# Turning token rows and gated rows on VectorE instead of TensorE in a mixture-of-experts feed-forward

## The chip, the cores and the metric

The kernel runs on one core of a Trainium2 chip. Its time is device microseconds of that core, from launch to end. Engines are TensorE (PE), VectorE (DVE), ScalarE (ACT), GpSimd (POOL) and SyncE (SP); each follows its own instruction stream, and they wait for each other on semaphores. DMAs issued from SP, ACT and POOL queues share 16 DMA engines.

## The reference

```python
def reference(x, ctx_2048, ...):                     # both (16, 512, 1024) fp32
    # long convolution of products k_i*k_j of 8-channel heads, contracted with the queries
    x = x + xattn(ctx, ctx, layernorm(x), ssm_kernel, D, 8)
    # mixture of experts: 32 routed experts, 8 of them per row, and a shared one
    h = layernorm(x).reshape(-1, 1024)               # T = 8192 token rows
    scores = sigmoid(h @ router_w)                   # (T, 32)
    # groups of 4 experts, 4 groups masked out, top 8 of the rest, weights scaled by 2.5
    gate = ragged_dot(xs, w_gate, group_sizes)       # xs: rows sorted by expert; w_gate (32, 1024, 512)
    up   = ragged_dot(xs, w_up, group_sizes)
    down = ragged_dot(silu(gate) * up, w_down, group_sizes)      # w_down (32, 512, 1024)
    routed = (down[unsort].reshape(T, 8, 1024) * weight).sum(1)
    shared = silu(h @ sw_gate) * (h @ sw_up) @ sw_down           # inner width 1024
    return x + routed + shared
```

## The kernel before, in words

Three parts run one after the other. `mix_and_route` computes the convolution and the router, and writes normed token rows to DRAM (`xnd`), the residual to `x2d`, and for each expert a list of its token numbers to `lists`. `plan` turns the counts into a table of tiles. `feed_forward` (L1009) does the rest, and only it is changed in its order of work.

It walks 672 tiles of 128 rows: 544 routed tiles (`EXPERT_TILES`), each of one expert, then twice 64 tiles of the shared expert, whose inner width is taken in two halves (`SH0`, `SH1`). The walk (`walk_tiles`, L988) is a few single tiles and loops of two. In tile t each engine also does work of its neighbours, so the stages overlap: the token rows of t+1 and t+2, the down product of t-1. The order is written out by hand in each engine's `tile`.

fp32 products are three passes (`three`, L1313): high with high, high with low, low with high, where the high part is a copy to fp32r and the low part is what is left. So every operand comes as a pair: whi and wlo of the weights (from `raw`), xhi and xlo of the token rows, hhi and hlo of the gated rows. ACT makes the high parts, DVE the low ones.

A tile goes like this. POOL loads the list row (`load_list`, L1109) and gathers 128 token rows into one of two `xg` buffers (`gather`, L1115). PE turns them with eight transposes into the PSUM tile xps (L1325); ACT and DVE make xhi and xlo from it (`x_high`, L1190, `x_low`, L1261). PE multiplies gate and up, 48 matmuls of 512 columns into gps and ups (L1336 to L1339). ACT applies silu (L1200), DVE multiplies with ups (L1282): the gated rows hb. PE turns them with four transposes into hps (L1358), ACT and DVE make hhi and hlo (L1212, L1299), and PE does the down product, 24 matmuls into yps, one tile later (L1349 to L1353). ACT and DVE copy yps to yrow, and POOL scatters it to `yd` (L1160).

PE's order within `tile(t)` is: gate and up of t, transposes of token rows t+1, down of t-1, transposes of gated rows t. ACT's is silu of t, x_high of t+1, the weight split of the next expert if t+1 is its first tile (`split_gu`, L1177), the copy of half of yps, hhi, and `split_dn`. DVE follows with the same pieces. Each expert's weights are 12 chunks in one `raw` buffer; SP loads the next expert's chunk once both engines have split the present one (L1068 to L1084).

In the 128 shared tiles `fetch_picks` (L1124) gathers four of a token's eight routed rows per tile into four `picked` buffers, `add_picks` (L1266) adds them to yrow with their weights, then yps is added (L1292), and ACT stores the sum (L1221).

## Time and profile before

| | us |
|---|---|
| median of 3 runs | 15433.22 (15427.76 to 15435.76) |
| the profiled execution, span from first to last instruction | 15412.0 |
| PE busy | 14528.9 (94%) |
| VectorE, ScalarE, GpSimd busy | 6313.4 (41%), 3173.3 (21%), 3896.2 (25%) |
| mean DMA rate | 94 GB/s |

The profile page gives no time of its own for the profiled execution beyond the span; the median of the runs lies 21 us above it. Busy shares are means over stages: the first 3,380 us are the convolution and the router, the rest is the feed-forward. A busy PE is a stream of matmuls whose starts lie close together; how long one occupies the array is read from the distance of starts, not from its own duration.

### The profile page before, as it was taken

The page shows a single profiled execution, that of the slowest core. Times are in us where ns is not written, and L with a number is a line of the kernel's source. Part 1 is how long each engine was busy: PE and PEld are TensorE (multiplying, and loading weights), DVE is VectorE, ACT ScalarE, POOL GpSimd, SP SyncE. Part 2 cuts the span into 40 slices and gives each one's busy share as a digit, 9 for nine tenths or more (in the row PEclk, how much of TensorE's full clock was granted, in tenths as well). Part 3 has the DMA queues.
Part 4 walks back from the last instruction along what each step waited for, and adds up shares of the span by engine and source line. Part 5 has one row for each costly group of instructions (what it writes and reads, how often), then busy time and mean ns, then how long its engine had stood idle before and what let it go on. Part 6 is the DMA issues. An engine that isn't in the chain of part 4 may idle for free.

```text
span 15412.0 us, 212654 instructions
## 1 busy us (share of the span) xinstructions
PE 14528.9 (94%) x73632; PEld 12344.4 (80%) x73633; DVE 6313.4 (41%) x7679; ACT 3173.3 (21%) x4006; POOL 3896.2 (25%) x3973
## 2 busy tenths in 40 slices
PE   7878877749999999999999999999999999999999
PEld 7777777738888888888888888788888888888888
DVE  8998989941221222212221222322212111444554
ACT  3333333311111112211211222312111111111111
POOL 3344445541111111111111111111111111333333
PEclk9888888869999999999999999999999999999999
DMA  2233332241221222212221222322212111666666
GB/s 69 69 63 66 66 64 63 53 72 60 74 75 59 74 76 105 91 60 73 91 74 58 91 89 91 129 93 102 73 60 75 58 60 42 210 206 204 208 204 204
DMA packets 481191, 1445.61 MB, mean 94 GB/s; under 512 B 94385, under 2 KB 94385, under 8 KB 480834
## 3 DMA queue, kind: packets, MB, share of 16 engines
q0 software_dynamic: 286720, 890.00, 17.3%
q1 hardware_dynamic: 172738, 485.33, 11.5%
q10 hardware_dynamic: 21504, 67.13, 1.1%
q8 instruction: 156, 2.56, 0.1%
q14 instruction: 73, 0.60, 0.0%
HBM read 1037.89 MB, written 421.08 MB: 95 GB/s over the span
## 4 chain that ended last, share of the span: by engine, by line
PE 77%; DVE 0%; DMA 0%; issue 0%; ACT 0%; DVEq 0%; ACTq 0%; SPq 0%; POOLq 0%; POOL 0%
PE gps L1318 24%; PE ups L1318 24%; PE yps L1318 24%; PE xps L1325 4%; PE hps L1358 2%; DVE wlo L1246 0%; DMA raw<-in_L_ffn_w_up_dram 0%; ACT whi L1181 0%; DMA xg<-xnd,idx 0%; DVE yrow L1272 0%; DMA picked<-yd,gidx 0%; ACTq L1063 0%; DVEq L1063 0%; DVE xlo L1246 0%; DVE hlo L1246 0%
## 5 line engine op out<-in xcount | busy, mean ns | idle before, releaser
L1282 DVE TENSOR_TENSOR hb<-hb,ups 128x512 f32<-128x512 f32 x672 | 462.1, 688 | 6196.1 <-ACT hb L1200 6196.1
L1160 POOL DMA_INDIRECT yd<-yrow,yidx x544 | 575.6, 1058 | 7816.9 <-DVE yrow L1296 7816.9
L1318 PE MATMUL gps<-whi,xhi 128*128 128x512 f32 x5376 | 2157.4, 401 | 32.8 <-DVE wlo L1246 29.1
L1318 PE MATMUL ups<-whi,xlo 128*128 128x512 f32 x5376 | 2112.9, 393 | 0.0
L1318 PE MATMUL gps<-wlo,xhi 128*128 128x512 f32 x5376 | 2111.6, 393 | 0.0
L1318 PE MATMUL ups<-whi,xhi 128*128 128x512 f32 x5376 | 2111.3, 393 | 0.0
L1318 PE MATMUL gps<-whi,xlo 128*128 128x512 f32 x5376 | 2110.9, 393 | 0.0
L1318 PE MATMUL ups<-wlo,xhi 128*128 128x512 f32 x5376 | 2094.3, 390 | 0.0
L750 PE MATMUL yps<-khi,thi 128*128 128x288 f32 x4608 | 1481.8, 322 | 337.7 <-ACT ysb L436 193.8
L1200 ACT ACTIVATE hb<-gps 128x512 f32<-128x512 f32 x672 | 402.4, 599 | 6729.3 <-PE ups L1318 6719.1
L1318 PE MATMUL yps<-whi,hhi 128*128 128x512 f32 x5376 | 1725.9, 402 | 4.5 <-DVE hlo L1246 4.5
L1318 PE MATMUL yps<-wlo,hhi 128*128 128x512 f32 x5376 | 1674.5, 393 | 0.0
L1318 PE MATMUL yps<-whi,hlo 128*128 128x512 f32 x5376 | 1666.7, 391 | 0.0
L750 PE MATMUL yps<-klo,thi 128*128 128x288 f32 x4608 | 1427.1, 310 | 0.0
L750 PE MATMUL yps<-khi,tlo 128*128 128x288 f32 x4608 | 1419.4, 308 | 0.0
L750 PEld LDWEIGHTS yps<-khi,thi 128*128 128x128 f32 x4608 | 934.9, 203 | 379.2 <-ACT ysb L436 215.9
L1318 PEld LDWEIGHTS gps<-whi,xhi 128*128 128x128 f32 x5376 | 1011.8, 188 | 234.8 <-DVE wlo L1246 30.1
L1318 PEld LDWEIGHTS yps<-whi,hlo 128*128 128x128 f32 x5376 | 1009.4, 188 | 230.3
L1318 PEld LDWEIGHTS ups<-wlo,xhi 128*128 128x128 f32 x5376 | 1010.2, 188 | 228.2
L1318 PEld LDWEIGHTS gps<-whi,xlo 128*128 128x128 f32 x5376 | 1010.7, 188 | 227.5
L1318 PEld LDWEIGHTS yps<-wlo,hhi 128*128 128x128 f32 x5376 | 1009.9, 188 | 222.1
L1318 PEld LDWEIGHTS gps<-wlo,xhi 128*128 128x128 f32 x5376 | 1011.4, 188 | 213.3
(161 smaller groups left out, 20294.0 us busy)
## 6 DMA issues: line engine op xcount, KB each, us to landing
raw<-in_L_ffn_w_gate_dram SPq DMA_DIRECT2D x128, 512.0 KB, 6.0
raw<-in_L_ffn_w_up_dram SPq DMA_DIRECT2D x128, 512.0 KB, 7.6
raw<-in_L_ffn_w_down_dram SPq DMA_DIRECT2D x64, 1024.0 KB, 6.9
cin<-in_ctx_dram SPq DMA_DIRECT2D x64, 512.0 KB, 5.0
xin<-in_x_dram SPq DMA_DIRECT2D x64, 512.0 KB
traw<-kpad SPq DMA_DIRECT2D x64, 512.0 KB, 4.2
xres<-in_x_dram SPq DMA_DIRECT2D x256, 128.0 KB, 2.6
x2d<-xres SPq DMA_DIRECT2D x64, 512.0 KB
```

Of the source, the lines that this page charges most:

```text
L750: last = pe.matmul(yps[j % 2][:, lb % 2, 0:NH], tt[sl][:, c], kk[half][:, lb - d, :], start=(d == 0 and i == 0), stop=(d == lb and i == 2))
L1160: pool.indirect_dma_start(out=yd, in_=yrow[i][:, :], in_offset=None, out_offset=bass.IndirectOffsetOnAxis(ap=yidx[i][:, 0:1], axis=0), bou ...
L1200: act.activation(hb[:, :], gps[:, :], ACT.Silu).then_inc(silu_done, 1)
L1282: dve.tensor_tensor(hb[:, :], hb[:, :], ups[:, :], ALU.mult).then_inc(h_done, 1)
L1318: ins = pe.matmul(ps, rows, w[:, chunk, i * 512:(i + 1) * 512], start=first and n == 0, stop=last_one and n == 2)
L1325: last = pe.transpose(xps[:, m * P:(m + 1) * P], xg[slot][:, m * P:(m + 1) * P], ident)
L1358: last = pe.transpose(hps[:, m * P:(m + 1) * P], hb[:, m * P:(m + 1) * P], ident)
```

## The change

The transposes leave PE. DVE turns each block of 32x32 of a tile (`dve.transpose`), which leaves the blocks where they were; the change brings the blocks to their places by other means.

For token rows: the rows of `xnd` are taken as four quarter rows of 256 columns. Partition group g (32 partitions) gathers quarter g of the tokens, and the four gathers of a tile fill the four groups of 32 tokens. List entries are stored as four times the token number, a load brings a list row to all four groups, and POOL adds the group number (`quad`) to it. After the block transpose (`x_turn`) into the SBUF tile `xt`, partition p holds columns of x in another order than before, and the host lays out the weights' rows to match (`weights`, `blocks_of_rows`). Gate and up come as one array, so a pair of chunks is one load of 1 MB, not two.

For gated rows: DVE turns hb into `ht`. ACT issues four DMAs that store `ht` to a DRAM tile `hsd` in pieces of 512 bytes (`spread_h`), then one that reads it back as `hz` with 2 KB a partition (`collect_h`). hhi and hlo are made from hz.

xps and hps are gone. The `picked` buffers go from four to two, so the third and fourth gather of a tile wait for the first and second addition. The order in `tile` changes too: x_high and x_low go ahead of silu and its product, POOL gathers the token rows ahead of the picks, and the tokens of t+2 are turned in tile t, not those of t+1.

```diff
-    c[:, C_TOK:C_TOK + RB] = p[:, None] + P * np.arange(RB)
+    c[:, C_TOK:C_TOK + RB] = QUADS * (p[:, None] + P * np.arange(RB))
...
+    c[:, C_POS] = QUADS * (p % SQ) + p // SQ
+    c[:, C_QUAD] = p // SQ
+    tokens = QUADS * np.arange(NTOK, dtype=np.int32)
+    tokens = tokens.reshape(NTILE, QUADS, SQ).transpose(0, 2, 1)
+    return c, np.ascontiguousarray(tokens).reshape(NTOK, 1)
...
+        sp.dma_start(raw[:, 2 * q:2 * q + 2, :], gate_up[:, 2 * q:2 * q + 2, :]).then_inc(w_ld[q], 16)
...
+    quarters = xnd.rearrange("n (a l) -> (n a) l", a=QUADS)
...
+        quad = sb("quad", [P, QUADS], I32)
+        idx = [sb(f"idx{i}", [P, QUADS], I32) for i in range(2)]
+        xidx = [sb(f"xidx{i}", [P, QUADS], I32) for i in range(2)]
...
-        xg = [sb(f"xg{i}", [P, L]) for i in range(2)]
+        xg = [sb(f"xg{i}", [P, QUADS, L // QUADS]) for i in range(2)]
+        xt = sb("xt", [P, KX, P])
         xhi, xlo = sb("xhi", [P, KX, P], F32R), sb("xlo", [P, KX, P], F32R)
         hb = sb("hb", [P, I])
+        ht = sb("ht", [P, I])
+        hz = sb("hz", [P, QUADS, KH, SQ])
...
         yrow = [sb(f"yrow{i}", [P, L]) for i in range(2)]
-        picked = [sb(f"picked{k}", [P, L]) for k in range(K // 2)]
+        picked = [sb(f"picked{k}", [P, L]) for k in range(2)]
 
         gps = es.enter_context(nc.psum_tensor("gps", [P, 512], F32))
         ups = es.enter_context(nc.psum_tensor("ups", [P, 512], F32))
-        xps = es.enter_context(nc.psum_tensor("xps", [P, 1024], F32))
-        hps = es.enter_context(nc.psum_tensor("hps", [P, 512], F32))
         yps = es.enter_context(nc.psum_tensor("yps", [P, 1024], F32))
...
-                wait(pool, x_ld[slot], 16 * turns)
-                pool.dma_start(idx[slot][:, :], lists[bass.ds(row * P, P), :]).then_inc(idx_ld[slot], 16)
+                wait(pool, x_ld[slot], 16 * QUADS * turns)
+                src = lists[bass.ds(row * P, P), :].rearrange("(o s q) n -> o s (q n)", o=1, q=QUADS)
+                pool.dma_start(idx[slot][:, :], src.to_broadcast([QUADS, SQ, QUADS])).then_inc(idx_ld[slot], 16)
 
             def gather(t, slot, turns):
 
-                wait(pool, xT_mm, t - 1 if not isinstance(t, int) else max(t - 1, 0))
+                wait(pool, x_turned, t - 1 if not isinstance(t, int) else max(t - 1, 0))
                 pool.wait_ge(idx_ld[slot], 16 * (turns + 1))
-                settle(pool, pool_turns)
-                pool.indirect_dma_start(out=xg[slot][:, :], out_offset=None, in_=xnd,
-                                        in_offset=bass.IndirectOffsetOnAxis(ap=idx[slot][:, 0:1], axis=0))\
-                    .then_inc(x_ld[slot], 16)
+                pool.tensor_tensor(xidx[slot][:, :], idx[slot][:, :], quad[:, :], ALU.add).then_inc(xidx_ready, 1)
+                pool.wait_ge(xidx_ready, t + 1)
+                for q in range(QUADS):
+                    settle(pool, pool_turns)
+                    pool.indirect_dma_start(out=xg[slot][:, q, :], out_offset=None, in_=quarters,
+                                            in_offset=bass.IndirectOffsetOnAxis(ap=xidx[slot][:, q:q + 1], axis=0))\
+                        .then_inc(x_ld[slot], 16)
...
                 for k in range(K // 2):
-                    if not isinstance(m, int) or m > 0:
-                        pool.wait_ge(pick_used, K // 2 * (m - 1) + k + 1)
+                    if not isinstance(m, int) or m > 0 or k > 1:
+                        pool.wait_ge(pick_used, K // 2 * m + k - 1)
                     settle(pool, pool_turns)
-                    pool.indirect_dma_start(out=picked[k][:, :], out_offset=None, in_=yd,
+                    pool.indirect_dma_start(out=picked[k % 2][:, :], out_offset=None, in_=yd,
                                             in_offset=bass.IndirectOffsetOnAxis(ap=gidx[slot][:, k:k + 1], axis=0))\
-                        .then_inc(pick_ld[k], 16)
+                        .then_inc(pick_ld[k % 2], 16)
...
             def tile(c):
-                if c.part(-1) is not None:
-                    fetch_picks(c.n(-1 - SH0), c.slot(-1 - SH0), c.part(-1))
                 if c.on(3):
                     load_list(c.n(3), c.slot(3), c.half(3))
                 if c.on(2):
                     gather(c.n(2), c.slot(2), c.half(2))
+                if c.part(-1) is not None:
+                    fetch_picks(c.n(-1 - SH0), c.slot(-1 - SH0), c.part(-1))
                 if c.part(-1) is None and c.on(-1):
...
             def x_high(t):
-                act.wait_ge(xT_mm, t + 1)
-                act.activation(xhi[:, :, :].rearrange("p k t -> p (k t)"), xps[:, :], ACT.Copy).then_inc(x_hi, 1)
+                act.wait_ge(x_turned, t + 1)
+                wait(act, gu_mm, t)
+                act.activation(xhi[:, :, :], xt[:, :, :], ACT.Copy).then_inc(x_hi, 1)
+
+            def spread_h(t, slot):
+
+                act.wait_ge(h_turned, t + 1)
+                for q in range(QUADS):
+                    act.dma_start(hsd[slot].rearrange("(b r) q x -> r b q x", r=SQ)[:, :, q, :],
+                                  ht[q * SQ:(q + 1) * SQ, :].rearrange("r (b x) -> r b x", x=P)).then_inc(h_st, 16)
+
+            def collect_h(t, slot):
+                act.wait_ge(h_st, 16 * QUADS * (t + 1))
+                wait(act, h_lo, t)
+                act.dma_start(hz[:, :, :, :].rearrange("p q k s -> p (q k s)"),
+                              hsd[slot].rearrange("p q x -> p (q x)")).then_inc(h_ld, 16)
 
             def tile(c):
                 t = c.n()
                 store_sum(c)
+                if c.on(1):
+                    x_high(c.n(1))
                 if c.on():
                     act.wait_ge(gu_mm, t + 1)
-                    wait(act, hT_mm, t)
+                    wait(act, h_turned, t)
                     act.activation(hb[:, :], gps[:, :], ACT.Silu).then_inc(silu_done, 1)
                 if c.on(1):
-                    x_high(c.n(1))
                     if c.part(-1) != 1:
                         with act.If(entry(act, c.n(1), F_FIRST, 1) == 1):
                             split_gu(entry(act, c.n(1), F_EXPERT, NE - 1))
+                if c.on():
+                    spread_h(t, c.slot())
                 if c.on(-1) and c.part(-1) is None:
                     act.wait_ge(down_mm, t)
                     wait(act, y_st[c.slot(-1)], 16 * c.half(-1))
                     act.activation(yrow[c.slot(-1)][:, 0:512], yps[:, 0:512], ACT.Copy).then_inc(y_act, 1)
                 if c.on():
-                    act.wait_ge(hT_mm, t + 1)
-                    act.activation(hhi[:, :, :].rearrange("p k t -> p (k t)"), hps[:, :], ACT.Copy).then_inc(h_hi, 1)
+                    collect_h(t, c.slot())
+                    act.wait_ge(h_ld, 16 * (t + 1))
+                    wait(act, down_mm, t)
+                    act.activation(hhi[:, :, :].rearrange("p k (q s) -> p q k s", s=SQ), hz[:, :, :, :], ACT.Copy)\
+                        .then_inc(h_hi, 1)
...
+            def x_turn(t, slot, turns):
+
+                dve.wait_ge(x_ld[slot], 16 * QUADS * (turns + 1))
+                wait(dve, x_lo, t)
+                dve.transpose(xt[:, :, :].rearrange("p k t -> p (k t)"),
+                              xg[slot][:, :, :].rearrange("p q (k r) -> p k q r", r=SQ)).then_inc(x_turned, 1)
+
             def x_low(t):
                 dve.wait_ge(x_hi, t + 1)
-                low(xlo[:, :, :].rearrange("p k t -> p (k t)"), xps[:, :],
-                    xhi[:, :, :].rearrange("p k t -> p (k t)")).then_inc(x_lo, 1)
+                low(xlo[:, :, :], xt[:, :, :], xhi[:, :, :]).then_inc(x_lo, 1)
...
-                    dve.wait_ge(pick_ld[k], 16 * (m + 1))
+                    dve.wait_ge(pick_ld[k % 2], 16 * (2 * m + k // 2 + 1))
                     at = K // 2 * half + k
                     dve.scalar_tensor_tensor(
-                        out=yrow[i][:, :], in0=picked[k][:, :],
+                        out=yrow[i][:, :], in0=picked[k % 2][:, :],
...
             def tile(c):
                 t = c.n()
+                if c.on(1):
+                    x_low(c.n(1))
                 if c.on():
                     dve.wait_ge(silu_done, t + 1)
                     dve.tensor_tensor(hb[:, :], hb[:, :], ups[:, :], ALU.mult).then_inc(h_done, 1)
+                    dve.wait_ge(h_done, t + 1)
+                    wait(dve, h_st, 16 * QUADS * t)
+                    dve.transpose(ht[:, :], hb[:, :]).then_inc(h_turned, 1)
                 if c.on(1):
-                    x_low(c.n(1))
                     if c.part(-1) != 1:
                         with dve.If(entry(dve, c.n(1), F_FIRST, 1) == 1):
                             split_gu(entry(dve, c.n(1), F_EXPERT, NE - 1))
+                if c.on(2):
+                    x_turn(c.n(2), c.slot(2), c.half(2))
                 i = c.slot(-1)
                 if c.part(-1) is not None:
...
                     dve.wait_ge(h_hi, t + 1)
-                    low(hlo[:, :, :].rearrange("p k t -> p (k t)"), hps[:, :],
-                        hhi[:, :, :].rearrange("p k t -> p (k t)")).then_inc(h_lo, 1)
+                    low(hlo[:, :, :].rearrange("p k (q s) -> p q k s", s=SQ), hz[:, :, :, :],
+                        hhi[:, :, :].rearrange("p k (q s) -> p q k s", s=SQ)).then_inc(h_lo, 1)
...
-            def transpose_rows(t, slot, turns):
-                pe.wait_ge(x_ld[slot], 16 * (turns + 1))
-                for m in range(KX):
-                    last = pe.transpose(xps[:, m * P:(m + 1) * P], xg[slot][:, m * P:(m + 1) * P], ident)
-                last.then_inc(xT_mm, 1)
...
                     last.then_inc(gu_mm, 1)
-                if c.on(1):
-                    transpose_rows(c.n(1), c.slot(1), c.half(1))
                 if c.on(-1):
...
                     last.then_inc(down_mm, 1)
-                if c.on():
-                    pe.wait_ge(h_done, t + 1)
-                    for m in range(KH):
-                        last = pe.transpose(hps[:, m * P:(m + 1) * P], hb[:, m * P:(m + 1) * P], ident)
-                    last.then_inc(hT_mm, 1)
...
+    A["hsd"] = nc.dram_tensor("hsd", (2, P, QUADS, P), F32).ap()
...
+def blocks_of_rows(w, chunks):
+    e, _, n = w.shape
+    return w.reshape(e, QUADS, chunks, SQ, n).transpose(0, 1, 3, 2, 4).reshape(e, P, chunks, n)
```

GpSimd, the loop over the first 64 shared tiles, one tile. `picked` are the routed rows, `idx` the list row, `xg` the token rows. Before:

```order
L1129 COPY gidx<-vslot 128x4
...
L1137 DMA picked<-yd,gidx 128x1024
...
L1137 DMA picked<-yd,gidx 128x1024
...
L1137 DMA picked<-yd,gidx 128x1024
...
L1137 DMA picked<-yd,gidx 128x1024
...
L1113 DMA idx<-lists 128x1
...
L1120 DMA xg<-xnd,idx 128x1024
```

After:

```order
L1120 DMA idx<-lists 128x1x4
...
L1126 TENSOR_TENSOR xidx<-idx,quad 128x4
L1130 DMA xg<-xnd,xidx 128x256 x4
...
L1139 COPY gidx<-vslot 128x4
...
L1147 DMA picked<-yd,gidx 128x1024 x2
...
L1147 DMA picked<-yd,gidx 128x1024
...
L1147 DMA picked<-yd,gidx 128x1024
```

The gathers now stand ahead of the picks, the one of token rows is four, and two of the four picks carry a wait between them.

ScalarE, the loop over routed tiles, one tile. hb is the gated rows, xhi the high part of token rows, whi that of weights (it runs only at a change of expert; x4 for gate and up, x2 for down), `hsd` the DRAM tile. Before:

```order
L1200 ACTIVATE hb<-gps 128x512
...
L1192 ACTIVATE xhi<-xps 128x1024
...
L1204 COMPARE_AND_BRANCH
...
L1181 ACTIVATE whi<-raw 128x2048 x4
...
L1209 ACTIVATE yrow<-yps 128x512
L1212 ACTIVATE hhi<-hps 128x512
...
L1216 COMPARE_AND_BRANCH
...
L1187 ACTIVATE whi<-raw 128x2048 x2
```

After:

```order
L1204 ACTIVATE xhi<-xt 128x1024
...
L1227 ACTIVATE hb<-gps 128x512
...
L1230 COMPARE_AND_BRANCH
...
L1192 ACTIVATE whi<-raw 128x2048 x4
...
L1210 DMA hsd<-ht 32x4x128 x4
...
L1237 ACTIVATE yrow<-yps 128x512
...
L1216 DMA hz<-hsd 128x512
...
L1242 ACTIVATE hhi<-hz 128x4x4x32
...
L1247 COMPARE_AND_BRANCH
...
L1198 ACTIVATE whi<-raw 128x2048 x2
```

xhi moved ahead of silu. Between the weight split and hhi there are now four stores, the copy of yps, and one load.

VectorE, the loop over the first 64 shared tiles, one tile. The branch with wlo is not taken there except at the change to the last set of weights. Before:

```order
L1282 TENSOR_TENSOR hb<-hb,ups 128x512
...
L1246 TENSOR_TENSOR xlo<-xps,xhi 128x1024
...
L1246 TENSOR_TENSOR wlo<-raw,whi 128x2048
...
L1272 SCALAR_TENSOR_TENSOR yrow<-picked,wpick,yrow 128x1024
...
L1272 SCALAR_TENSOR_TENSOR yrow<-picked,wpick,yrow 128x1024
...
L1272 SCALAR_TENSOR_TENSOR yrow<-picked,wpick,yrow 128x1024
...
L1272 SCALAR_TENSOR_TENSOR yrow<-picked,wpick,yrow 128x1024
...
L1292 TENSOR_TENSOR yrow<-yrow,yps 128x1024
L1246 TENSOR_TENSOR hlo<-hps,hhi 128x512
```

After:

```order
L1277 TENSOR_TENSOR xlo<-xt,xhi 128x1024
...
L1321 TENSOR_TENSOR hb<-hb,ups 128x512
...
L1324 STREAM_TRANSPOSE ht<-hb 128x512
...
L1277 TENSOR_TENSOR wlo<-raw,whi 128x2048
...
L1296 STREAM_TRANSPOSE xt<-xg 128x1024
...
L1309 SCALAR_TENSOR_TENSOR yrow<-picked,wpick,yrow 128x1024
...
L1309 SCALAR_TENSOR_TENSOR yrow<-picked,wpick,yrow 128x1024
...
L1309 SCALAR_TENSOR_TENSOR yrow<-picked,wpick,yrow 128x1024
...
L1309 SCALAR_TENSOR_TENSOR yrow<-picked,wpick,yrow 128x1024
...
L1335 TENSOR_TENSOR yrow<-yrow,yps 128x1024
L1277 TENSOR_TENSOR hlo<-hz,hhi 128x4x4x32
```

xlo moved ahead of the product with ups, and two block transposes stand ahead of the four additions of picked rows.

## Rows read from the trace of the kernel before

**Rows 1.** Busy time by stretch: window, length, busy us of each engine, clock, DMA.

```profile
3380.00:13100.00 9720.00, 9687.60 (x45606) 8011.87 (x45607) 2203.67 (x2360) 1816.11 (x2361) 1570.85 (x2172) 1.00 0.22 77
13100.00:15412.00 2312.00, 2300.13 (x10835) 1901.97 (x10833) 1160.67 (x1040) 308.47 (x400) 772.95 (x896) 1.00 0.62 206
```

**Rows 2.** The page's chain that ended last, shares of the span by line.

```profile
PE gps L1318 24%; PE ups L1318 24%; PE yps L1318 24%; PE xps L1325 4%; PE hps L1358 2%; DVE wlo L1246 0%; DMA raw<-in_L_ffn_w_up_dram 0%; ACT whi L1181 0%; DMA xg<-xnd,idx 0%; DVE yrow L1272 0%; DMA picked<-yd,gidx 0%; ACTq L1063 0%; DVEq L1063 0%; DVE xlo L1246 0%; DVE hlo L1246 0%
```

**Rows 3.** Waits of PE in the feed-forward, the largest: total us, times, longest.

```profile
PE gps L1318 <- DVE wlo L1246: 29.1, 3, 10.5
```

**Rows 4.** Timeline of PE, one routed tile: start us, length us, instruction.

```profile
9005.96 1.03 PE L1325 MATMUL xps<-con_sb,xg 128*128 128x128 f32 x8
9006.75 0.71 PE L1318 MATMUL yps<-whi,hhi 128*128 128x512 f32 x2
...
9012.34 0.60 PE L1358 MATMUL hps<-con_sb,hb 128*128 128x128 f32 x4
9012.70 0.48 PE L1318 MATMUL gps<-whi,xhi 128*128 128x512 f32 x1
9013.02 0.39 PE L1318 MATMUL ups<-whi,xhi 128*128 128x512 f32 x1
...
9023.55 0.40 PE L1318 MATMUL ups<-whi,xlo 128*128 128x512 f32 x1
9023.78 1.04 PE L1325 MATMUL xps<-con_sb,xg 128*128 128x128 f32 x8
```

**Rows 5.** Timelines of ScalarE and VectorE, the same tile.

```profile
9006.24 0.60 ACT L1200 ACTIVATE hb<-gps 128x512 f32<-128x512 f32 x1 [10.43 <-PE ups L1318]
...
9013.75 0.69 DVE L1246 TENSOR_TENSOR hlo<-hps,hhi 128x512 fp32r<-128x512 f32 x1 [0.41 <-ACT hhi L1212]
```

**Rows 6.** Timelines: ScalarE's queue in the last stretch, GpSimd in the routed one.

```profile
13616.47 0.35 ACTq L1229 DMA_DIRECT2D shd<-yrow  x1
...
9032.05 1.03 POOL L1160 DMA_INDIRECT yd<-yrow,yidx  x1 [14.54 <-DVE yrow L1296]
...
9034.36 0.97 POOL L1120 DMA_INDIRECT xg<-xnd,idx  x1 [0.30 <-issue]
```

**Rows 7.** DMA issues of the whole span: count, KB each, median us to landing.

```profile
raw<-in_L_ffn_w_up_dram SPq DMA_DIRECT2D x128, 512.0 KB, 7.6
...
xres<-in_x_dram SPq DMA_DIRECT2D x256, 128.0 KB, 2.6
...
shd<-yrow ACTq DMA_DIRECT2D x64, 512.0 KB, 6.7
...
idx<-lists POOLq DMA_DIRECT2D x672, 0.5 KB, 3.1
xg<-xnd,idx POOLq DMA_INDIRECT x672, 4.3
yd<-yrow,yidx POOLq DMA_INDIRECT x544, 3.4
```

**Rows 8.** Timelines of PE, ScalarE and VectorE at a change of expert.

```profile
6392.69 0.50 PE L1318 MATMUL gps<-whi,xhi 128*128 128x512 f32 x1
...
6388.39 7.33 ACT L1181 ACTIVATE whi<-raw 128x2048 fp32r<-128x2048 f32 x4 [0.37 <-issue]
...
6390.34 8.90 DVE L1246 TENSOR_TENSOR wlo<-raw,whi 128x2048 fp32r<-128x2048 f32 x4 [1.07 <-ACT whi L1181]
```

**Rows 9.** Timelines of VectorE and GpSimd in a shared tile.

```profile
13609.34 1.29 DVE L1272 SCALAR_TENSOR_TENSOR yrow<-picked,wpick,yrow 128x1024 f32<-128x1024 f32 x1
...
13611.82 1.09 POOL L1137 DMA_INDIRECT picked<-yd,gidx  x1 [0.82 <-POOL gidx L1129]
...
13617.00 0.59 POOL L1113 DMA_DIRECT2D idx<-lists  x1
```

**Rows 10.** DMA issues from 13,200 to 14,200 us: count, median us to landing.

```profile
picked<-yd,gidx POOLq DMA_INDIRECT x225, 6.3
...
xg<-xnd,idx POOLq DMA_INDIRECT x56, 7.2
```

78 lines of the change are left out of this document (43 added, 35 removed).

## The prediction

> **What bounds the kernel now.** I read the busy time by stretch first [rows 1]. The feed-forward runs from about 3,380 us to the end, 12,032 of the 15,412 us of the span. In both of its stretches PE (TensorE) is busy over 99% at a granted clock of 1.00, the upper of its two levels (2.4 GHz), while VectorE is busy 23% of the routed stretch and 50% of the last one, and the DMA engines 22% and 62%. The chain that ended last says the same [rows 2]: the three products hold 24% of the span each, the transposes of token rows (xps) 4% and those of gated rows (hps) 2%, and no other engine's line reaches 1%. In the view of waits, the largest of PE in the whole feed-forward is 29.1 us in total, in 3 places [rows 3]. So PE's own instruction stream sets the pace, and everything else has slack. What the change takes from that stream is gain until something else is late.
>
> **What leaves PE.** In the timeline of one steady tile [rows 4] the gate-up product ends at 9005.96 (the zero of all offsets below), eight transposes hold PE until 9006.75 (0.79 us), the down product until 9012.34, four transposes until 9012.70 (0.36 us), and the next gate-up product ends at 9023.78: 17.82 us a tile. Within a product the matmuls start 0.229 us apart (9013.02 to 9023.55 is 46 steps). 72 matmuls at that step make 16.49 us. The difference, 1.33 us, is 1.15 us of transposes and 0.18 us of the wider step at the first matmul behind each block of them (9012.70 to 9013.02 is 0.32 us). Whether the wider step stays at a switch of product the trace can't say: the saving is 1.15 to 1.33 us, and I take 1.25, a period of 16.57 us. Over the 544 routed tiles that is 680 us.
>
> **What is added beside it, and whether it is late.** The down product of tile t starts when gate-up of t+1 ends, at +16.5. Before, its operand hlo was there at +8.5, and silu started at +0.28 [rows 5]. Now it goes: x_high first on ScalarE (+0.3 to +1.3; the 1,024 elements at half the 1.83 us of a 2,048 element split come to 0.9, twice silu's 0.60 to 1.2; I take 1.0), silu to +1.9, x_low on VectorE to +2.5 (1.11 us, half of a wlo of 2,048 elements, 8.90 us for four, also of two SBUF operands [rows 8]), the product with `ups`, 0.69 us like hlo, to +3.2. The block transpose of 512 elements is in no row; it lies between the 0.60 us of an activation of that size and twice the 0.69 us of a product of it; I take 0.7: +3.9. The transpose of token rows likewise 1.2 (1.2 to 2.4), off this path. Then four DMA issues on ScalarE's queue at 0.35 us, the time of one shd issue [rows 6]; the last starts at +5.0. Landing of a store of four parts: 2.6 us (four 128 KB loads) to 6.7 us (a shd store) [rows 7]. The read back: 3.1 us (the smallest load, idx) to 7.6 us (a weight load in its burst); I take 3.4, near idx, since it is 256 KB on a quiet queue. Adding 0.2 us for its issue, 0.60 for hhi, 0.69 for hlo and 0.3 for three hand-overs, hlo is there at +12.8 (5.0 + 2.6 + 0.2 + 3.4 + 1.6). Cover is left: 3.7 us. In the routed stretch the cost of the round trip is nothing, and I take that.
>
> The Trainium skill speaks against the edit at this point: VectorE: DVE Perf Modes, The three transpose paths, rates one 128x128 bf16 transpose at 390 ns on TensorE and 311 ns on VectorE, the latter in 32x32 blocks only, and its rules for kernel authors send a full 128x128 to TensorE if PSUM will do. For TensorE the rows differ: eight in 0.79 us, 0.10 us each. By the Trainium skill's figure for VectorE the two transposes would be an estimated 2.5 and 1.2 us a tile, which would put hlo at +13.3 instead of +12.8, still covered in the routed stretch.
>
> GpSimd, in the routed stretch: four gathers for one, 3 x (0.97 + 0.30) = 3.8 us, plus an addition with its wait, 1.0 us; it waits 14.5 us a tile now for yrow [rows 6]. Hidden. Were they not, the token transpose would be late on VectorE.
>
> **Expert changes**, 34 sets of weights (32 experts and two halves of the shared one), 33 of them inside the stream. There PE waits little today: at 6385.92 gate-up ends, wlo starts at 6390.34 and its first unit of 2.2 us is ready at about 6392.6, just as PE is back from its down product and transposes (6392.69) [rows 8]. Two things change. First, the transposes no longer cover: down ends at +5.5, the whi split starts at +2.3 (behind x_high and silu), its first unit is low at +6.6: 1.1 us of waiting. Second, on ScalarE the four h stores stand behind the whi split (7.33 us), so they are issued at +9.6 to +11.0 instead of +3.9. hlo then comes at 11.0 + store + 0.35 + load + 1.6; with 2.6 and 3.1 that is +18.7, with 6.7 and 6.0, a little under a weight load, +25.7, against a PE that is ready at +17.6. The raw weight loads of the next expert run just then and land in up to 7.6 us [rows 7], so neither end is excluded; the middle is 4.6 us. Together 5.7 us a change (2.2 to 9.2), 33 times: 188 us (73 to 304).
>
> **The 128 tiles that also sum.** VectorE now has behind the two transposes (+5.2) four multiply-adds of 1.29 us [rows 9], but only two `picked` buffers: k2 is fetched once k0 is added, k3 once k1 is. On GpSimd the loop is closed [rows 6, 9]: from the end of k0's addition k2 is issued by 1.5 us, k3 by 2.9, idx by 3.5, the index addition by 4.6, four gathers by 9.5, gidx and its gap to 10.6, then k0 of the next tile starts and lands L later, and is added in 1.3. The loop is 11.9 us + L. L was 4.3 us for a gather in the routed stretch, 6.3 for a pick in a burst of four and 7.2 for the xg gather behind that burst [rows 7, 10]. With 0.5 MB of h traffic a tile added to 3.7 MB (206 GB/s for 17.8 us) at a DMA share of 62% [rows 1] I take 5.5, near the middle of 4.3 and 6.3: 17.4 us a tile. VectorE's chain agrees: k3 issued +8.2, landed +13.7, added +15.0, the sum with yps +16.2, hlo +16.9, 0.4 us late. So 0.42 us is saved per tile, 54 us in all (170 with L of 4.3, a loss of 164 with 7.2).
>
> **Loads.** Gate and up of a chunk pair come as one load of 1 MB with 8 KB a partition instead of two of 512 KB, the same bytes. Weights made PE wait 29.1 us in all [rows 3]; I leave that as it is (0 to 29 us of gain). The idx load grows from 0.5 to 2 KB, a tile ahead of its use.
>
> **Ends.** The first tile has one gather and transpose more ahead of it, and behind the last gate-up the round trip is bare: 12.8 - 5.5 us. 15 us.
>
> **The sum**: 680 - 188 + 54 - 15 = 531 us off the profiled span of 15,412, and the median lies 21 us above that span: 15,412 - 531 + 21 = 14,902. I forecast 14,900.
>
> **Rivals.** (a) Most cover holds: landings at an expert change are at the low end (73 us), gathers take 4.3 us in the sums (170), and the wide step goes too (724): 806 us less, 14,627. For it: the DMA engines are 78% free in the routed stretch. Against: the weight loads fall on just that moment. (b) The sums become DMA-bound: L is 7.2 or more, the loop 19.1, 164 us lost: 680 - 188 - 164 - 15 = 313, so 15,120. For it: 62% DMA share before, and 1 KB and 512 B pieces now. (c) Slower: the trip of h through DRAM is late in every tile. Landings of 6.7 and 7.2 us put hlo at +20.6, 4.1 us late; a late down product delays the next-but-one gate-up, so every second tile pays and the period is 18.6, 0.75 us over today's: 15,433 + 672 x 0.75 + 188 + 15 = 16,140. It begins to cost at landings of 9.7 us together and eats the whole gain, expert changes counted, from about 12 us. For it: stores of 512 KB took 6.7 us; against: that was at 62% DMA share, and the routed yd scatter, 512 KB as well, landed in 3.4. The fixed part of a DMA bears on it: the Trainium skill, DMA: Bandwidth & Descriptors, puts it at about 2 us per DMA, most of it the receipt of the last write, and advises against DMAs under 64 KB; the four h stores are 64 KB each. The rows agree with it so far (idx, 0.5 KB, 3.1 us [rows 7]). (d) The edit does not do what it says on PE: the transposes had covered the table reads and waits between the products, which cost ScalarE 0.37 us between xhi and whi [rows 8]. With two such gaps bare the saving is 1.33 - 0.74 = 0.6 us a tile, and none in the sums: 326 - 188 - 15 = 123, 15,310.
>
> **Chances.** Forecast 0.50 (its own range 14,780 to 15,030), (a) 0.20, (b) 0.16, (c) 0.08, (d) 0.06. The range 14,640 to 15,230 takes the forecast, (b) and most of (a). A measurement of this kernel tells about 0.2% from no change. Faster 0.88 (all but (c) and a worse (d)), the same 0.03, slower 0.09.
>
> **What would show it.** PE with 72 matmuls a tile and a start-to-start of a tile of 16.5 to 16.6 us in the routed stretch; no wait of yps for hlo there outside expert changes; at these, waits of gps for wlo near 1 us and of yps for hlo of some 5 us; in the last stretch a tile of 17 to 18 us, PE waiting for hlo, and VectorE waiting for picked. The forecast is wrong if hlo is late in a plain routed tile (c), if the tile is 17.2 us with no wait shown (d), or if a block transpose takes over twice the copy of its size.

## The result and the profile after

The changed kernel takes 15,456.9 us (median of 20 runs, 15,439.6 to 15,470.3) against 15,430.9 us of the kernel before (20 runs): a ratio of 1.0017 [1.0011, 1.0023]. I had forecast 14,900 us and a range of 14,640 to 15,230. So it is no faster, but 0.17% slower.

Busy time by stretch of the kernel after (columns as in [rows 1]):

```profile
3380.00:12757.00 9377.00, 9186.58 (x39215) 7390.84 (x39216) 3237.14 (x3465) 1864.52 (x2373) 3515.18 (x4367) 0.99 0.36 112
12757.00:15457.00 2700.00, 2310.77 (x9170) 1819.29 (x9168) 1375.02 (x1283) 291.39 (x390) 1346.30 (x1392) 0.93 0.64 199
```

The routed stretch got shorter (9,377 us for 9,720), the stretch that also sums longer (2,700 for 2,312), and in the latter PE is idle for 390 us, where it was idle for 12, at a mean clock of 0.93 where [rows 1] has 1.00. To place the border exactly I take three starts of a gate-up product: the first, the first one in which sums run beside it, and the last. PE's timeline before, and after:

```profile
3381.43 0.80 PE L1318 MATMUL gps<-whi,xhi 128*128 128x512 f32 x1 [2.37 <-DVE xlo L1246]
...
13131.54 0.48 PE L1318 MATMUL gps<-whi,xhi 128*128 128x512 f32 x1
...
15379.08 0.48 PE L1318 MATMUL gps<-whi,xhi 128*128 128x512 f32 x1
```

```profile
3399.12 0.80 PE L1366 MATMUL gps<-whi,xhi 128*128 128x512 f32 x1 [133.09 <-DVE xlo L1277]
...
12757.25 0.40 PE L1366 MATMUL gps<-whi,xhi 128*128 128x512 f32 x1
...
15412.20 0.40 PE L1366 MATMUL gps<-whi,xhi 128*128 128x512 f32 x1
```

The stages between them, all in us; the last two columns are versions met below, read the same way:

| | before | forecast | after | after, old step | four buffers |
|---|---|---|---|---|---|
| start of the feed-forward | 3,381 | +15, both ends | 3,399 | 3,400 | 3,398 |
| routed part | 9,750 | 9,258 | 9,358 | 9,209 | 9,361 |
| 127 tiles with sums | 2,248 | 2,194 | 2,655 | 2,633 | 2,133 |
| from the last gate-up to the end | 33 | | 46 | 48 | 36 |
| span | 15,412 | 14,881 | 15,458 | 15,291 | 14,928 |

The routed part gave 392 us, 100 less than forecast. The tiles with sums took 407 us more, where I had 54 less. With 18 and 13 us at the ends that is the +46 of the span.

**A plain routed tile.** PE (answering to [rows 4]), then ScalarE and VectorE ([rows 5]), after:

```profile
9016.18 0.63 PE L1366 MATMUL yps<-whi,hhi 128*128 128x512 f32 x2
...
9021.78 0.40 PE L1366 MATMUL gps<-whi,xhi 128*128 128x512 f32 x1
9022.01 0.40 PE L1366 MATMUL ups<-whi,xhi 128*128 128x512 f32 x1
...
9032.98 0.63 PE L1366 MATMUL yps<-whi,hhi 128*128 128x512 f32 x2
```

```profile
9016.38 1.06 ACT L1204 ACTIVATE xhi<-xt 128x1024 fp32r<-128x1024 f32 x1 [6.55 <-PE ups L1366]
9017.34 0.58 ACT L1227 ACTIVATE hb<-gps 128x512 f32<-128x512 f32 x1
9020.18 1.80 ACTq L1210 DMA_DIRECT2D hsd<-ht  x4
...
9023.44 0.35 ACTq L1216 DMA_DIRECT2D hz<-hsd  x1
9026.07 0.63 ACT L1242 ACTIVATE hhi<-hz 128x512 fp32r<-128x512 f32 x1 [3.36 <-DMA hz<-hsd]
...
9017.47 1.22 DVE L1277 TENSOR_TENSOR xlo<-xt,xhi 128x1024 fp32r<-128x1024 f32 x1 [6.92 <-ACT xhi L1204]
...
9019.44 0.71 DVE L1324 STREAM_TRANSPOSE ht<-hb 128x512 f32<-128x512 f32 x1
9020.55 1.25 DVE L1296 STREAM_TRANSPOSE xt<-xg 128x1024 f32<-128x1024 f32 x1 [0.41 <-issue]
...
9026.73 0.69 DVE L1277 TENSOR_TENSOR hlo<-hz,hhi 128x512 fp32r<-128x512 f32 x1 [3.96 <-ACT hhi L1242]
```

The round trip goes as forecast: the block transposes take 0.71 and 1.25 us (0.7 and 1.2), hlo is there 11.2 us behind the gate-up product (12.8), and the next one ends at +16.8. The change does on PE what it says: 72 matmuls and nothing else. But the tile is 16.80 us (9016.18 to 9032.98), not 16.57: gate-up is 48 matmuls in 11.20 us (9021.78 to 9032.98), one every 0.2333 us. Before it was 0.229. The extra gap at the switch of products is gone, and the step is wider everywhere, at a granted clock of 1.00 in both.

**A tile with sums.** PE, GpSimd and VectorE, after (GpSimd's answer to [rows 6], VectorE's to [rows 9]):

```profile
14019.32 0.39 PE L1366 MATMUL ups<-whi,xlo 128*128 128x512 f32 x1
14024.78 1.22 PE L1366 MATMUL yps<-whi,hhi 128*128 128x512 f32 x2 [5.07 <-DVE hlo L1277]
14025.79 1.06 PE L1366 MATMUL yps<-wlo,hhi 128*128 128x512 f32 x2
...
14014.50 1.40 POOL L1147 DMA_INDIRECT picked<-yd,gidx  x1 [5.48 <-DVE yrow L1309]
14016.20 0.94 POOL L1147 DMA_INDIRECT picked<-yd,gidx  x1 [0.30 <-issue]
14017.45 0.75 POOL L1120 DMA_DIRECT2D idx<-lists  x1 [0.31 <-issue]
...
14023.91 0.94 POOL L1130 DMA_INDIRECT xg<-xnd,xidx  x1 [0.30 <-issue]
...
14025.93 2.00 POOL L1147 DMA_INDIRECT picked<-yd,gidx  x1 [0.88 <-POOL gidx L1139]
...
14012.36 1.28 DVE L1309 SCALAR_TENSOR_TENSOR yrow<-picked,wpick,yrow 128x1024 f32<-128x1024 f32 x1 [1.62 <-DMA picked<-yd,gidx]
...
14032.93 1.28 DVE L1309 SCALAR_TENSOR_TENSOR yrow<-picked,wpick,yrow 128x1024 f32<-128x1024 f32 x1 [2.71 <-DMA picked<-yd,gidx]
```

From one addition of k0 (14012.36) to the next (14032.93) it is 20.6 us. The loop that I had written down is there: addition 1.3 us, end of it to the issue of the next k0 12.3 (14013.64 to 14025.93), landing 7.0 (14025.93 to 14032.93). I had 1.3, 10.6 and 5.5. These are the terms of one tile; over 123 tiles of the stretch the same starts and ends give 1.3, 13.7 and 6.1 on average, 21.0 us together. So most of the excess is GpSimd's round (13.7 for 10.6) and little of it the landing (6.1 for 5.5). Up to the end of k3's issue the round takes 4.7 us on average where I had 2.9: k3 waits until k1 is added, and that addition ends 2.7 us behind that of k0, not 1.4 as two additions in a row would. From there to the first gather of tokens it is 2.3 us (1.7), and the four gathers take 5.5 (4.9).

PE stands for 5.1 us in this tile (3.1 on average, by the view of waits below), and then pays again: the first matmuls behind this pause run at the lower clock level (1.2 GHz). Two windows behind the pause (the last three numbers are clock, DMA share and GB/s):

```profile
14024.80:14029.20 4.40, 4.40 (x10) 3.44 (x11) 2.76 (x4) 1.52 (x2) 3.19 (x4) 0.50 0.65 189
14030.00:14034.00 4.00, 4.00 (x19) 3.23 (x18) 1.29 (x2) 0.00 (x0) 0.00 (x0) 1.00 0.99 360
```

Ten matmuls at 0.43 us instead of 0.23 are 2 us. Not every pause is followed by this: of 123 pauses in the stretch 78 are, with 1.9 us each. A tile of 20.9 us is 16.8 of matmuls, 2.9 of pauses and 1.1 of the lower clock.

The waits of PE, VectorE and GpSimd from 12,757 us to the end:

```profile
PE yps L1366 <- DVE hlo L1277: 374.0, 121, 10.3
...
DVE yrow L1309 <- DMA picked<-yd,gidx: 963.7, 415, 5.8
...
POOL picked L1147 <- DVE yrow L1309: 891.1, 196, 11.3
```

PE waits for VectorE, VectorE for the pick, and GpSimd, before it fetches the pick, for VectorE: a closed loop with PE outside it. And PE's waits in the routed part (to [rows 3]):

```profile
PE yps L1366 <- DVE wlo L1277: 88.2, 10, 13.4
PE gps L1366 <- DVE wlo L1277: 79.1, 32, 12.4
```

### The profile page after: what moved, and what is told of

It is laid out like the page before. It is cut to its first block, busy times and chain, and to the rows that moved or that the text cites. A ratio compares the mean times of both kernels' runs of the same rounds, so it can differ in the third digit from the quotient of the medians.

```text
span 15457.8 us, 210467 instructions
## 1 busy us (share of the span) xinstructions
PE 14036.3 (91%) x65568; PEld 11637.5 (75%) x65569; DVE 7555.5 (49%) x9027; ACT 3200.2 (21%) x4006; POOL 6410.3 (41%) x6661
## 4 chain that ended last, share of the span: by engine, by line
PE 56%; DMA 7%; issue 7%; DVE 3%; POOL 3%; ACT 1%; POOLq 1%; ACTq 0%; DVEq 0%; SPq 0%
PE gps L1366 19%; PE ups L1366 19%; PE yps L1366 18%; DMA picked<-yd,gidx 5%; POOL xg L1130 2%; DVE yrow L1309 1%; DVE wlo L1277 1%; DMA hsd<-ht 1%; POOL picked L1147 1%; DMA hz<-hsd 0%; ACT xhi L1204 0%; DVE xlo L1277 0%; DVE hb L1321 0%; DMA raw<-in_w_gu_dram 0%; POOLq L1072 0%
## 5 line engine op out<-in xcount | busy, mean ns | idle before, releaser
L1130 POOL DMA_INDIRECT xg<-xnd,xidx x2688 | 2853.0, 1061 | 1205.3 <-issue 632.8
L1277 DVE TENSOR_TENSOR xlo<-xt,xhi 128x1024 fp32r<-128x1024 f32 x672 | 823.2, 1225 | 3681.7 <-ACT xhi L1204 3482.4
L1366 PE MATMUL yps<-whi,hhi 128*128 128x512 f32 x5376 | 1770.0, 412 | 466.2 <-DVE hlo L1277 374.0
L1366 PE MATMUL ups<-wlo,xhi 128*128 128x512 f32 x5376 | 2131.0, 396 | 0.0
L1366 PE MATMUL yps<-wlo,hhi 128*128 128x512 f32 x5376 | 1743.8, 407 | 0.0
L1366 PE MATMUL yps<-whi,hlo 128*128 128x512 f32 x5376 | 1739.8, 406 | 0.0
L1366 PEld LDWEIGHTS yps<-whi,hhi 128*128 128x128 f32 x5376 | 1041.7, 196 | 768.8 <-issue 427.7
L1204 ACT ACTIVATE xhi<-xt 128x1024 fp32r<-128x1024 f32 x672 | 712.1, 1060 | 4294.8 <-PE ups L1366 3202.7
L1277 DVE TENSOR_TENSOR hlo<-hz,hhi 128x512 fp32r<-128x512 f32 x672 | 466.1, 694 | 2010.3 <-ACT hhi L1242 1992.4
L1366 PEld LDWEIGHTS yps<-wlo,hhi 128*128 128x128 f32 x5376 | 1050.0, 195 | 256.6
```

The costliest lines, as they stand in the source:

```text
L1130: pool.indirect_dma_start(out=xg[slot][:, q, :], out_offset=None, in_=quarters, in_offset=bass.IndirectOffsetOnAxis(ap=xidx[slot][:, q:q + ...
L1204: act.activation(xhi[:, :, :], xt[:, :, :], ACT.Copy).then_inc(x_hi, 1)
L1277: return dve.tensor_tensor(dst, src, hi.bitcast(F32), ALU.subtract)
L1366: ins = pe.matmul(ps, rows, w[:, chunk, i * 512:(i + 1) * 512], start=first and n == 0, stop=last_one and n == 2)
```

## The experiments

Three questions: what makes the sums' tiles long, what makes PE's step wide, and what an expert change costs. All ratios are to the kernel before on the same chip. A step is the mean distance of starts within a product.

**1. Two sum buffers in the kernel before** (`picked`, its semaphores and waits as in the changed kernel).

```
-        picked = [sb(f"picked{k}", [P, L]) for k in range(K // 2)]
+        picked = [sb(f"picked{k}", [P, L]) for k in range(2)]
```

> The kernel before with one part of the change: two picked buffers instead of four, the third and fourth pick wait for the first and second addition; all else as before, transposes on TensorE. Theory (the two buffers alone close a loop: issue, landing L, addition 1.3, twice a tile): with L of 6 to 7 us the 128 shared tiles take 2 x (0.9 + L + 1.3) + about 1 = 17.5 to 19.5 us instead of 17.8, so the kernel is 0 to 210 us slower, near 100. Rival (the loss needs the four gathers on GpSimd in the same loop): 17.8 us a shared tile, 15,431, no change.

15,442.3 us, 1.0012 [1.0003, 1.0022]; the tiles with sums stay at 17.82 us, and only the one at the change to the last weights takes 26.5 us where it took 20.0. In the kernel before, two buffers alone cost nearly nothing: with its one gather of tokens and its order of work the loop closes in under 17.8 us.

**2. The changed kernel with whole token rows in one gather** (tokens reach the product in a wrong order).

```
-                for q in range(QUADS):
-                    ... out=xg[slot][:, q, :] ... in_=quarters ...
+                ... out=xg[slot] (whole row), in_=xnd, one index ...
```

> The changed kernel with one gather of whole 4 KB rows per tile instead of four of quarter rows; it leaves out the placing of quarters in partition groups, so the token operand is in the wrong order. It takes 3.8 us off GpSimd's loop in the shared tiles. Theory (loop through GpSimd of 12.3 + L + 1.3 us, L 7.0): the shared tile goes from 21 us to the next bound, the two-buffer loop of about 18.4, 128 x 2.6 = 330 us less, 15,125. Rival (landing time L of the picks alone, DMA-bound): the tile stays above 20 us, under 130 us less. Second rival, on the routed tiles: if quarter gathers cost nothing there, their 16.80 us stay.

15,202.4 us, 0.9857 [0.9841, 0.9874]. The routed part keeps its 16.80 us tile (9,366 us); the tiles with sums fall from 20.9 to 18.8 us (2,392 for 2,655). Three gathers of 1.25 us each less in the loop would give 3.8 us; over half of it shows. The rest of the way down to 16.80 us does not come, and here GpSimd waits for VectorE longer than in the changed kernel (1,239 us for 891), so that its own work is no longer what fills the loop. From 12,760 us to the end of this run:

```profile
POOL picked L1146 <- DVE yrow L1308: 1238.8, 239, 16.6
```

**3. The changed kernel with four sum buffers again.** There is no SBUF left for them, so two lie in the last two chunks of `raw`, and the last load of weights waits for the last sum.

```
+        picked += [raw[:, KX + KH - 2 + k, :] for k in range(2)]
-                    if not isinstance(m, int) or m > 0 or k > 1:
-                        pool.wait_ge(pick_used, K // 2 * m + k - 1)
+                    if not isinstance(m, int) or m > 0:
+                        pool.wait_ge(pick_used, K // 2 * (m - 1) + k + 1)
```

> The changed kernel with four picked buffers again, two of them in the last two chunks of raw, whose last load waits until the first 64 shared tiles have been summed. Quarter gathers and the trip of h through DRAM stay. Theory (buffers closed the loop): GpSimd has about 13 us of work in a shared tile and no loop, so the tile falls from 21 to about 17 us (16.8 at best), 128 x 4 = 510 us less, 14,950. Rival (DMA-bound at 62 to 66% share, h late): the tile stays at 19 us or more, under 260 us less, 15,200 or more.

14,929.9 us, 0.9680 [0.9663, 0.9696]. Its last stretch, and what PE still waits for there:

```profile
12760.00:14928.00 2168.00, 2146.34 (x9164) 1726.20 (x9162) 1368.70 (x1283) 291.27 (x389) 1232.87 (x1390) 0.99 0.76 248
```

```profile
PE yps L1373 <- DVE hlo L1284: 14.4, 3, 5.4
```

The same transfers now run at 248 GB/s, a DMA share of 0.76, and PE is not held: 2,133 us, 16.79 a tile. So the sums are not bound by the DMA engines (rival (b) falls); the loop that closes through two buffers is what cost 522 us in these tiles (2,655 to 2,133). Four gathers with four buffers cost nothing that shows (16.79 us a tile). With two buffers they are about half of it, 263 us by run 2; the other 259 stay with a single gather, though two buffers cost the kernel before nothing (run 1). VectorE has two turns more a tile than in run 1 (0.71 and 1.25 us) and the order of work is another; which of these makes the second half, no run isolates.

**4 to 7. Candidates for the step.** In the changed kernel pads that put the operands at 32 modulo 64 bytes again, as before; in the four buffer version the old PSUM banks for `yps`, and one TensorE transpose of constants a tile; in the kernel before no TensorE transposes (from the third tile the products take stale rows).

```
+        sb("pad1", [P, 8])                                        (4, and pad0 ahead of raw)
+        es.enter_context(nc.psum_tensor("dps0", [P, 1024], F32))  (5, and dps1 of 512)
+        pe.transpose(dps[:, 0:P], con[:, C_ID:C_ID + P], con[:, C_ID:C_ID + P])   (6)
-        for m in range(KX): last = pe.transpose(xps..., xg..., ident)             (7)
+        pe.sem_inc(xT_mm, 1)
```

> The changed kernel with 32 unused bytes a partition ahead of raw and 32 behind wlo, so that raw, whi and wlo start at 32 modulo 64 bytes, as they did in the kernel before, instead of at 0. Theory (the start-to-start of matmuls, 0.2333 us instead of 0.2289, comes from where the moving operand lies): it goes back to 0.229, the routed tile from 16.80 to 16.49 us, 544 x 0.31 = 170 us less, 15,290. Rival (the pitch comes from the load on TensorE or on SBUF without the transposes' pauses, or from PSUM): 0.2333 stays and the time is 15,457.

> e3_four_buffers (14,930) with three PSUM banks left unused between ups and yps, so that yps lies in the banks where it lay before the change. Theory (the step of 0.2333 us comes from the banks): 0.229 in the down product or in both, 60 to 200 us less. Rival (not the banks): no change, 14,930.

> e3_four_buffers (14,930) with one TensorE transpose of a constant 128x128 per tile, into a PSUM bank that nobody reads, between the gate-up and the down product. Open: why matmuls start 0.2333 us apart in the changed kernel and 0.2289 before. Theory (the transposes between the products are what made the step shorter): it goes back to 0.229, the tile from 16.80 to 16.49 + 0.1 to 0.2, 670 x 0.15 = 100 us less, 14,830. Rival (not the transposes): the step stays 0.2333 and the transpose costs 0.1 to 0.2 us a tile, 70 to 130 us more, 15,030.

> The kernel before without its TensorE transposes except those of the first two tiles: token and gated operands are made again and again from what then stands in xps and hps, so the products are of old rows; all other engines do the work of before. It gives the most that taking the transposes off TensorE can bring. Theory (the step depends on the transposes' absence): the tile is 72 x 0.2333 = 16.80 us, 670 x 1.02 = 685 us less than before, 14,740. Rival (the step of 0.2289 belongs to the old kernel's other parts): 72 x 0.2289 = 16.49, 890 us less, 14,530.

Run 4: 15,451.7 us, 1.0017 [1.0007, 1.0027], step 0.233. Run 5: 14,946.5 us, 0.9683 [0.9667, 0.9699] (run 3 has 0.9680), step 0.233. Run 6: 15,009.2 us, 0.9725 [0.9708, 0.9741], tile 16.90, step 0.233. So far nothing but misses. Run 7: 14,567.5 us, 0.9435 [0.9420, 0.9451]; tile 16.48 us, and the step is 0.229 without any transpose. So the pauses of the transposes did not make the old step short; something else of the old program does. It also bounds what leaving them out can bring with nothing added and the operands where they were: 869 us.

**8. The kernel before with the operands moved** to exactly the changed kernel's places in SBUF (pads, and two `picked` buffers allocated earlier).

```
+        sb("pad1", [P, 24])
+        picked = [sb("picked0", [P, L])]
         ...
+        picked += [sb("picked1", [P, L])]
```

> The kernel before, with a few pads and two of the sum buffers placed earlier in SBUF, so that the weights' two parts and both tokens' and gated rows' parts (whi, wlo, xhi, xlo, hhi, hlo) stand at exactly the addresses that they have in the changed kernel. If these addresses make the changed kernel's wider step between matmuls (0.2333 us in place of 0.229), the step widens here: 72 x 0.0043 = 0.31 us on each of 672 tiles, 210 us, a tile of 18.13 us and some 15,640 us. If they don't, step and time stay: 0.229, 17.82 and 15,430 us.

15,607.9 us, 1.0116 [1.0099, 1.0133]. Two pairs of one product, PE's timeline of run 8, and before:

```profile
9013.44 0.63 PE L1321 MATMUL yps<-whi,hhi 128*128 128x512 f32 x2
9013.91 0.63 PE L1321 MATMUL yps<-wlo,hhi 128*128 128x512 f32 x2
9014.38 0.40 PE L1321 MATMUL yps<-whi,hlo 128*128 128x512 f32 x1
```

```profile
9009.59 0.62 PE L1318 MATMUL yps<-whi,hhi 128*128 128x512 f32 x2
9010.05 0.62 PE L1318 MATMUL yps<-wlo,hhi 128*128 128x512 f32 x2
9010.51 0.39 PE L1318 MATMUL yps<-whi,hlo 128*128 128x512 f32 x1
```

Four matmuls in 0.94 us here and in 0.92 there (over a whole product 0.233 and 0.229), in the same instructions. The tile is 18.09 us for 18.13, and 178 of the 210 us came. The step is a matter of places. Run 4 had looked at the wrong property of them.

**9. The kernel before with the changed kernel's loads of weights.**

```
-        for src, c in ((gate, 0), (up, I)):
-            sp.dma_start(raw[:, 2 * q:2 * q + 2, c:c + I], src[...].rearrange("(k p) i -> p k i", p=P))
+        sp.dma_start(raw[:, 2 * q:2 * q + 2, :], gate_up[:, 2 * q:2 * q + 2, :]).then_inc(w_ld[q], 16)
```

> The kernel before with only the changed kernel's way of loading weights: they lie in DRAM as each partition's rows behind one another, gate and up side by side, one DMA a unit where gate-up had two (in the order of channels of the kernel before). TensorE's transposes stay. If the step of 0.2333 us comes from the weights (their layout or their DMAs), it shows here and the time is about 15,640 us. If it comes from elsewhere, 0.229 and about 15,430 us (within 15 us).

15,428.5 us, 0.9999 [0.9990, 1.0009]: this part of the change costs and brings nothing.

**10. The map of places.** One matmul 24 times in a row for each of 400 pairs of places.

```
for n in range(12):
    for ps in (gps, ups):
        pe.matmul(ps[:, :], rows[j][:, 0:P], weights[i][:, 0:512], start=n == 0, stop=n == 11)
```

> Nothing of the kernel but its matmul: one stationary operand (128x128) and one moving operand (128x512), both f32r, 24 matmuls in a row into two banks in turn, for each of 400 pairs of places in SBUF. The moving operand stands at 32 x i bytes (i = 0 to 15, and for three places of the other one 16 to 63, past a multiple of 2048), the stationary one at 32 x j past a multiple of 512. The rest of the computation is left out. In the kernel before the places are i = 31, j = 5, in the changed one i = 32, j = 9, in the version with operands at 32 modulo 64 i = 33, j = 11. If the step depends on the two places' distance (the weight load of the next matmul beside the stream of this one), it is 0.229 us at i = 31, j = 5 and wherever the distance is the same, and 0.233 at the other two. If it depends on one operand's place alone, whole rows or whole columns of the map are alike. If the cause lies in other tiles that only moved along, all pairs have the same step, and the addresses stay without an explanation.

The first matmul of a pair and that of the next pair, 24 steps apart, on PE's timeline; wbn, wbp, wca, wcb are i = 29, 31, 32, 33, and xaf, xaj, xal are j = 5, 9, 11:

```profile
1630.53 0.39 PE L64 MATMUL gps<-wbn,xaf 128*128 128x512 f32 x1
...
1635.99 0.40 PE L64 MATMUL gps<-wbo,xaf 128*128 128x512 f32 x1
...
1641.60 0.40 PE L64 MATMUL gps<-wbp,xaf 128*128 128x512 f32 x1
...
1647.10 0.40 PE L64 MATMUL gps<-wca,xaf 128*128 128x512 f32 x1
...
1914.70 0.40 PE L64 MATMUL gps<-wca,xaj 128*128 128x512 f32 x1
...
1920.30 0.39 PE L64 MATMUL gps<-wcb,xaj 128*128 128x512 f32 x1
...
2187.88 0.40 PE L64 MATMUL gps<-wcb,xal 128*128 128x512 f32 x1
...
2193.49 0.40 PE L64 MATMUL gps<-wcc,xal 128*128 128x512 f32 x1
```

Divided by 24, which is good to 0.0004 us: 0.2275 us (distance of rows from weights 0 modulo 256 bytes), 0.2292 (192, the kernel before), 0.2333 (32, the changed kernel) and 0.2338 (64, run 4). Over all pairs but the very first, which starts at the lower clock, the step follows from that distance alone: 0.2267 to 0.2280 at 0, 0.2287 to 0.2293 at 192, 0.2324 to 0.2341 at the six others. The map is one execution; the runs below try it in the kernel. The kernel before stood, by chance of its allocation, at the second best of eight. Three small new buffers between the weights' and the rows' parts (`quad` and two `xidx`, 32 bytes each) moved the changed one off it; the new constants lie ahead of both and moved both alike.

**11 to 13. Places chosen by the map**: the four buffer version at distance 0, the changed kernel as it is at 192, the kernel before at distance 0.

```
+        sb("pad", [P, 56])       (11; 40 in 12, 16 in 13)
         xhi, xlo = sb("xhi", [P, KX, P], F32R), sb("xlo", [P, KX, P], F32R)
```

> The version with four sum buffers, and 224 bytes of pad ahead of xhi, so that the rows' parts stand at a whole multiple of 256 bytes from the weights' parts, where the map has its shortest step (0.2267 to 0.2277 us). If the map carries over: 72 x 0.0056 to 0.0066 = 0.40 to 0.48 us off each of 672 tiles, a tile of 16.35 to 16.42 us and 14,930 - 270 to 320 = 14,610 to 14,660 us. Rival: in the kernel the four pairs of operands take turns and the sums' gathers and the expert changes are the next bound, so that the step shortens but less than half of it shows: 14,780 us or more.

> The changed kernel itself (two sum buffers) with 160 bytes of pad ahead of xhi: the distance of rows and weights modulo 256 is that of the kernel before (192), for which the map has 0.2293 us. The step should be 0.229, a routed tile 16.49 us, 544 x 0.31 = 169 us off the routed tiles. Theory: the 128 shared tiles are held by the closed loop of two sum buffers and stay at about 21 us each, so 15,457 - 170 = 15,287 us. Rival: the shared tiles go by PE's clock and step too, and 0.31 x 128 = 40 us more go: 15,247 us or less.

> The kernel before with 64 bytes of pad ahead of xhi: rows' and weights' parts a whole multiple of 256 bytes apart. By the map 0.0016 to 0.0026 us off each of 72 matmuls, 0.11 to 0.19 us off a tile of 17.82 us, 75 to 125 us in all: 15,305 to 15,355 us. If the places matter only where the step was wide, it stays at 15,430 us.

Run 11: 14,641.1 us, 0.9490 [0.9474, 0.9506], a tile of 16.32 us: the best version, 5.1% under the kernel before. Run 12: 15,294.4 us, 0.9915 [0.9898, 0.9931]; routed tile 16.48, tiles with sums 20.7 on average (2,633 us for 127): 163 us for 160 bytes of pad, 149 of them in the routed part. The tiles with sums gave 22 us, where a loop through PE would have given 39; single runs of the changed kernel lie up to 31 us apart, so the 22 us are not clear of noise, and fit a loop without PE in it. Run 13: 15,372.6 us, 0.9966 [0.9953, 0.9978], tile 17.74. The times of the first two fell within what the map gave; the third is 17 us above its range: its step is 0.2278 us, where run 11 at the same distance has 0.2267. Why it got only half of the way is open.

**14 to 16. Expert changes**, in the four buffer version: without the turns and the trip (tokens and gated rows go unturned into the products), the down weights split ahead of the gated rows' parts, and the h stores and load between the units of the gate-up split.

```
-                dve.transpose(ht[:, :], hb[:, :]).then_inc(h_turned, 1)          (14, and xt, hsd, hz)
+                split_dn(...)   ahead of   act.wait_ge(h_ld, ...), and of hlo    (15)
+                unit(0); spread_h(t, c.slot()); unit(1); ...; unit(2); collect_h; unit(3)   (16)
```

> The version with four sum buffers, without VectorE's block transposes of token and gated rows and without the trip of the gated rows through DRAM: the rows go unturned into the products (that part of the computation is left out), the quarter gathers stay. PE's instructions are the same. If the turns or the trip (VectorE's or the DMAs' work beside PE) make the step of 0.2333 us, it is 0.229 here, a tile 16.49 us, and the time 14,930 - 208 = 14,720 us or less; what is shorter still is the cover that the turns took at expert changes (up to 80 us). If the step belongs to something else, it stays and the time is 14,850 to 14,930 us, by the expert changes alone.

> The version with four sum buffers, and in the first tile of an expert the down weights are split (ScalarE and VectorE) ahead of the gated rows' two parts, while these are on their trip, and not behind them. Theory: of the 162 us that expert changes cost more than in the kernel before, the waits of the down product for its weights' lower part (88 us in 10 places) come from the split standing behind the trip: they fall to under 30 us and the time to about 14,870 us. Rival: the split then makes the gated rows late, the down product waits for hlo in its place at up to 33 changes, and the time is 14,930 to 14,980 us.

> e3_four_buffers (14,930) with ScalarE's order at a change of expert changed: the four stores of gated rows stand behind the first of the four whi units, the load behind the third. In the changed kernel the changes of expert cost 220 us of tile time above 16.80, before 53. Theory (the h stores stand behind 7.3 us of weight splitting, so hlo and the split of the down weights are late): hlo comes at about +15 instead of +22, no wait for hlo or for wlo of the down product is left, about 110 us less, 14,820. Rival (landing times under the weight loads, or the split itself, decide): under 40 us less.

PE's waits in the routed part, run 14, then run 15:

```profile
PE gps L1345 <- DVE wlo L1269: 39.0, 32, 10.9
```

```profile
PE yps L1373 <- DVE hlo L1284: 94.4, 30, 11.2
PE gps L1373 <- DVE wlo L1284: 62.1, 30, 8.1
```

Run 14: 14,774.0 us, 0.9575 [0.9559, 0.9591]; the tile keeps 16.80 us and the step 0.233 (as its places are unchanged), and the routed part is 9,213 us, 148 less than in run 3. That is what turns and trip cost at expert changes; of the 156 us between the two runs 8 are left for all else. Run 15: 14,936.4 us, 0.9681 [0.9665, 0.9697]: the wait for the weights' lower part was exchanged for one of the same size for hlo; my theory fell. Run 16: 14,958.5 us, 0.9691 [0.9675, 0.9707], no gain either. My reading, which no run isolates: gated rows and next weights need ScalarE and VectorE in the same few microseconds, whatever their order.

## Why the prediction was wrong

- *What leaves PE.* 1.25 us a tile, 680 us. The count of instructions was right, and the wider gap at a switch of products did go, as in rival (a). But the sum took for granted that the 0.229 us of [rows 4] belong to the matmul. They belong to its operands' places, and the change moved those: 0.31 us a tile, 149 us in the routed part and 163 in all by run 12. With the old step a tile is 16.48 us. The profile before has this step only, so it could not show it, but the step should have been a term with a bound of its own.
- *Whether the added work is late.* Right in mechanism and size: hlo at +11.2 for 12.8, no wait for it in plain tiles. Rival (c) did not come, and neither did (d): there is no bare gap between products, the time over 16.57 us is the step. The estimate worked out from the Trainium skill's bf16 figure for VectorE (VectorE: DVE Perf Modes, The three transpose paths) was 2.5 and 1.2 us for the two turns; the trace has 1.25 and 0.71 for fp32. The Trainium skill's advice in Rules for kernel authors of the same page, to leave a full 128x128 to TensorE, would not have been the best here: eight TensorE transposes held the bounding engine for 0.79 us, VectorE's 1.25 us lie on an engine that waits, and with four sum buffers (run 3) the version without them is 3.2% faster than the kernel before.
- *Expert changes.* 188 us forecast. What the routed tiles take above a plain one rose from 56 us to 219, so by 163; by run 14 turns and trip cost 148 of it. The size is right, what waits for what is not: I had named hlo as what comes late, and it is the lower part of the weights, gate-up's at 32 changes (2.5 us each, where I had 1.1) and down's at 10. Run 15 shows that this is only a matter of order.
- *The 128 tiles that also sum.* This is the step that failed. The loop was the right one, but its terms were too small: "The loop is 11.9 us + L", with L of 5.5, and it is 15.0 + 6.1 on average (13.6 + 7.0 in the tile shown). The term that failed most is GpSimd's round, 13.7 us where I had 10.6. I let k3 follow k2 at once, "k2 is issued by 1.5 us, k3 by 2.9", though k3 waits until k1 is added, and k1 is added late, which makes 1.3 of the 3.1 us. Most of the rest is issue time: some gathers take 1.4 to 2.0 us there, where I had 1.09 and 0.97. L was 0.6 us over my value, and inside its range. So 17.4 us a tile became 20.9, 461 us over the 127 tiles, which by itself is more than the range allowed for. Every microsecond in a closed loop counts in full, 128 times. The time at the lower clock behind PE's pauses doesn't come on top: PE is outside the loop. A second bound lay above 17.4 us as well, though the chain of VectorE that I wrote down seemed to agree: with a single gather the tile is still 18.8 us (run 2). Rival (b), a loop of 19.1 us by an L of 7.2, was nearer in size and wrong in its cause: it said DMA-bound, and run 3 moves the same bytes in 2,133 us.

The rest closes: with the old step (run 12) the span is 410 us over the forecast's 14,881; the tiles with sums are 439 of it, the routed part 49 less, the two ends 19 more.

## What to carry to other kernels

When a change makes room by halving a ring of buffers, write the loop that closes through it with every engine's issue time in the loaded stretch, not the quiet one; if its sum comes within a few microseconds of the tile, keep the ring, and look for its room elsewhere, as in buffers that are idle in that stretch (527 us here, of which fewer gathers in the loop gave back only half). And write down the wait for every buffer of the ring, not for the first alone. Before blaming or crediting an edit for a change of a few per cent in a matmul's step, look at where the allocator put its two operands: one pad was worth 163 us in the changed kernel, 289 us in the version with four buffers and some 57 us in the kernel before.

## What the runs showed of the hardware

The step from one 128x128 by 128x512 matmul (f32r) to the next, with the stationary operand loaded anew each time, depends on the distance of the two operands in a partition modulo 256 bytes: 0.2267 to 0.2280 us at 0, 0.2287 to 0.2293 at 192, and 0.2324 to 0.2341 at all others, at a granted clock of 1.00 (run 10, one execution). In the kernels it was 0.2267 at 0 (run 11; but 0.2278 in run 13), 0.229 at 192 (before, run 12) and 0.233 at 32 and 64 (after, run 4). Why 192 and not 64 is second is open. TensorE came back from a pause of 5 us at a granted clock of 0.50, the lower level of 1.2 GHz, and was at 1.00 again some 5 us later; 78 of 123 pauses in that stretch had such slow matmuls behind them. GpSimd's gathers took 0.94 to 2.00 us in one tile; that VectorE's work beside them is the cause was not tried.
